# Two-layer block (state-space layer, then FFN): running the FFN of tile t-2 inside the state-space work of tile t

## What is computed

```python
x = x + layernorm(mamba(layernorm(x), W_in, conv_w, conv_b, W_out, A_log, D_param, dt_bias))
x = x + layernorm(ffn(layernorm(x), lut, gate_idx, up_idx, down_idx))

# mamba: proj = u @ W_in.T, split into z, x, B, C, dt
#   xBC = silu(causal_conv(xBC, 4 taps) + conv_b);  dt = softplus(dt + dt_bias);  dA = exp(dt * A)
#   per token: S = S * dA + dt * outer(B, x);  y = S @ C       (8 heads, state 64)
#   y = (y + D_param * x) * silu(z);  return y @ W_out.T
# ffn: w = lut[idx] for three weights (16 levels);  h = silu(x @ gate.T) * (x @ up.T)
#   return h @ down.T                                          (width 512, inner width 1376)
```

## Time and profile before

| | us |
|---|---|
| median of the runs | 1591.49 (1589.11 to 1592.44) |
| span of the profiled execution | 1590.2 |
| TensorE busy | 1431.8 (90%) |
| VectorE busy | 1034.1 (65%) |
| ScalarE busy | 592.3 (37%) |
| GpSimd busy | 541.7 (34%) |

### The profile page before, as it was taken

How to read it: one execution, slowest core, us unless ns; L and a number is a source line. 1 busy time by engine, 2 the same in 40 slices (tenths; PEclk the granted TensorE clock), 3 DMA queues, 4 the chain that set the end, 5 groups by cost and what they waited for, 6 DMA issues and landing times. The chain is left out here.

```text
span 1590.2 us, 23447 instructions
## 1 busy us (share of the span) xinstructions
PE 1431.8 (90%) x7392; PEld 707.9 (45%) x7392; DVE 1034.1 (65%) x2288; ACT 592.3 (37%) x1046; POOL 541.7 (34%) x653
## 2 busy tenths in 40 slices
PE   3798897898979988899886999999999999999998
PEld 1354443443535434445443444444444444444443
DVE  6799797897886978969885535435363545445333
ACT  4365554654645546555453221203020221213020
POOL 1275655556465555665754001010101001010101
PEclk9899998998999999989998999999999999999999
DMA  5011122022121221112201101010100101010000
GB/s 168 1 49 49 49 62 64 15 72 59 38 63 36 62 62 49 59 39 62 62 22 59 53 9 46 1 55 1 54 1 21 34 7 47 1 53 1 27 1 27
DMA packets 37454, 65.22 MB, mean 41 GB/s; under 512 B 5056, under 2 KB 15296, under 8 KB 37312
## 3 DMA queue, kind: packets, MB, share of 16 engines
q1 hardware_dynamic: 35424, 63.47, 12.7%
q10 hardware_dynamic: 1888, 0.03, 0.1%
HBM read 46.71 MB, written 16.78 MB: 40 GB/s over the span
## 5 line engine op out<-in xcount | busy, mean ns | idle before, releaser
L1386 ACT ACTIVATE gtanh<-bank,c_gate_half 128x512 f32<-128x512 f32 (+1 forms) x88 | 60.4, 687 | 537.0 <-PE bank L1421 537.0
L1421 PE MATMUL bank<-xt,ffn_hi 128*128 128x512 f16 (+1 forms) x704 | 213.8, 386 | 13.4 <-DVEq L82 6.7
L991 DVE TENSOR_SCALAR mask<-codes_h 128x416 f16<-128x416 f16 x640 | 215.5, 368 | 1.9
L1421 PE MATMUL bank<-xt_odd,ffn_hi 128*128 128x512 f16 (+1 forms) x704 | 209.4, 379 | 0.0
L1359 POOL TENSOR_TENSOR drstd<-dvar,neg_half 128x1 f32<-128x1 f32 x32 | 17.4, 545 | 481.1 <-DVE dvar L1518 481.1
L828 PE MATMUL bank<-mask,diag 128*128 128x416 f16 x640 | 133.2, 353 | 46.8 <-DVE mask L991 46.6
L1493 DVE SCALAR_TENSOR_TENSOR gsilu<-gtanh,bank 128x512 f32<-128x512 f32 (+1 forms) x88 | 60.5, 687 | 137.6 <-ACT gtanh L1386 137.4
L1421 PE MATMUL bank<-xt,ffn_lo 128*128 128x512 f16 (+1 forms) x352 | 135.7, 385 | 0.0
L1445 PE MATMUL bank<-ffn_hi,h_hi 128*128 128x512 f16 (+1 forms) x352 | 133.5, 379 | 0.0
L1421 PE MATMUL bank<-xt_odd,ffn_lo 128*128 128x512 f16 (+1 forms) x352 | 133.4, 379 | 0.0
L1445 PE MATMUL bank<-ffn_hi,h_lo 128*128 128x512 f16 (+1 forms) x352 | 133.3, 379 | 0.0
(11 more groups left out here) (184 smaller groups left out, 2768.3 us busy)
## 6 DMA issues: line engine op xcount, KB each, us to landing
codes_sb<-codes SPq DMA_DIRECT2D x80, 208.0 KB, 3.5
ut<-u SPq DMA_DIRECT2D x8, 1024.0 KB, 5.7
ures<-u SPq DMA_DIRECT2D x32, 256.0 KB, 2.7
x_scratch<-x SPq DMA_DIRECT2D x32, 256.0 KB, 2.0
xf<-x_scratch SPq DMA_DIRECT2D x8, 1024.0 KB, 5.9
out<-res SPq DMA_DIRECT2D x32, 256.0 KB, 2.0
ffn_hi<-w_in_t SPq DMA_DIRECT2D x4, 580.0 KB, 10.3
ffn_hi<-w_out_t SPq DMA_DIRECT2D x1, 1024.0 KB, 14.5
```

Source lines behind the costliest of these rows:

```text
L991: ins = nc.vector.tensor_scalar(mask[:, n, q, :], codes_h[:, n, :], float(2 * q), None, ALU.is_equal)
L1386: gtanh_ready.inc(nc.scalar.activation(gtanh[0:w, m % 2, :], banks[2 + m % 2][0:w, :], ACT.Tanh, scale=c_gate_half[0:w, :]))
L1421: last = nc.tensor.matmul(bank, wt[:, c0:c0 + w], xts[i][:, half, k, :], start=(k == 0 and n == 0), stop=(k == KC - 1 and n == 2))
```

## The change

The two stages become one. There are ten steps: in step t < 8 the state-space layer of tile t runs, and from t = 2 on the FFN of tile g = t-2 (`LAG = 2`) runs between its parts; steps 8 and 9 (`tail`) are the FFN alone. The 40 units of codes (now 20 in each of steps 0 and 1, each 64 rows of 832 columns) are decoded in the first two steps, with 8 masks of 832 columns a unit. The number of matmuls and of their columns is the same. The order of all queues is written out for each step; no loops are left.

- The conversion of the codes goes from GpSimd to ScalarE (`codes_to_half`, with a bias in place of the lowering on VectorE). The z gate goes from GpSimd and three ScalarE operations to one ScalarE tanh and one VectorE operation (`z_gate`).
- The layer norm of FFN input slices uses the same code as that of `u` (normalise and high part on ScalarE, low part on VectorE); slices are loaded and normalised in pairs.
- Gate, up and down products of the FFN share three banks (3, 6, 7) in strict turns; a turn may start once the turn three before it has been read (`ffn_turn`). The state-space layer keeps banks 0, 1, 2, 4, 5.
- x1 has one buffer; the residual of the FFN is loaded chunk by chunk.
- The end of chunk 3 of a tile (`out_rstd`, `normalise`, `add_residual`) and of the last down product stands in the next step.

In the diff the four `stage` functions are, in this order, those of TensorE, VectorE, GpSimd and ScalarE, each cut to its beginning.

```diff
+LAG = 2
+FFN_BANKS = (3, 6, 7)
+FFN_TURNS = 2 * MB + SUB
...
+                def gate_up(g, m):
...
+                    for side, col0, done in ((0, GATE0, gate_done), (1, UP0, up_done)):
+                        turn = 2 * m + side
+                        if turn < 3:
+                            pe.wait_ge(ffn_turn.sem, ffn_turn.prev(g, (FFN_TURNS - 1, FFN_TURNS, FFN_TURNS)[turn]))
+                        else:
+                            pe.wait_ge(ffn_turn.sem, ffn_turn.now(g, turn - 2))
+                        bank = banks[FFN_BANKS[turn % 3]][0:w, :]
...
+                def stage(t):
+                    scan(t, 0)
+                    if dec:
+                        decode(t, 0)
+                    if ffn:
+                        gate_up(g, 0)
+                        gate_up(g, 1)
+                    if nxt:
+                        slice_transpose(t, "T0")
+                        slice_transpose(t, "T1")
+                    prepare(t, 1)
+                    segment_sums(t, 1)
+                    if dec:
+                        decode(t, 1)
+                    if ffn:
+                        gate_up(g, 2)
+                    transpose_y(t, 0)
...
+                    scan(t, 1)
+                    if dec:
+                        decode(t, 5)
+                    if nxt:
+                        project_dt(t + 1)
+                        project_conv(t + 1, 4)
+                    if ffn:
+                        gate_up(g, 5)
+                    prepare(t, 2)
+                    segment_sums(t, 2)
...
+                    if nxt:
+                        project_z(t + 1, 3)
+                    if dec:
+                        decode(t, 19)
+                    if ffn:
+                        down(g, 3)
...
+                def stage(t):
+                    y_sum(t, 0)
+                    if g >= 1:
+                        down_stats(g - 1, 3)
+                    if t >= 1:
+                        out_stats(t - 1, 3)
+                    if g >= 1:
+                        down_normalise(g - 1, 3)
+                    if ffn:
+                        gate_silu(g, 0)
+                    y_gated(t, 0)
+                    if ffn:
+                        times_up(g, 0)
+                    y_split(t, 0, k + 2 if dec else None)
...
+                def stage(t):
+                    decay_state(t, 0)
+                    if t >= 1:
+                        out_rstd(t - 1, 3)
+                    if g >= 1:
+                        down_rstd(g - 1, 3)
+                    if t >= 1:
+                        add_residual(t - 1, 3)
+                    segments(t, 1)
+                    if g >= 1:
+                        add_output(g - 1, 3)
+                    weights(t, 1)
...
+                def stage(t):
+                    if dec:
+                        codes_to_half(k + 4)
+                    if ffn:
+                        gate_tanh(g, 0)
+                    if nxt:
+                        normalise_slice("u", t + 1, 0, 0)
+                        normalise_slice("u", t + 1, 0, 1)
+                    if ffn:
+                        high(g, 0)
+                        gate_tanh(g, 1)
...
+                    if nxt:
+                        slice_transposed(t, "T0", xt)
+                        slice_transposed(t, "T1", xt)
+                    if t >= 1:
+                        normalise(t - 1, 3)
+                    small(t, 1)
```

More of the change, by code:

```diff
@@ L1 @@
+from collections import namedtuple
 from contextlib import ExitStack
@@ new lines, in sandwich_kernel, with place, pair_buffer, pair_landed @@
+        res_stored = [Signal(sem(f"output_stored{i}"), SUB // 2, step=16, credit=True) for i in range(2)]
+        def place(t, name):
+            b, n = place_of[t, name]
+            return Place(banks[b], shared_filled[b], shared_freed[b], n)
+        def pair_buffer(no):
+            return xs[:, 1, 0:2, :] if no == 1 else ut[:]
+        def pair_landed(no):
+            return u_loaded[1].sem if no == 1 else u_loaded[0].sem, 16 * (no if no > 1 else 1)
+        def conv_sum(i, f):
+            return xs[:, i % HALVES, 0 if f == KC else f, :]
@@ L917, in body @@
                         pe.wait_ge(s_diag, 2 * PAIRS)
                         pe.wait_ge(s_lo, len(PIECES))
-                        decode(t, 0, more)
-                        transpose_y(t, 0)
-                        input_transpose(t, 0, more)
-                        input_transpose(t, 1, more)
-                        scan(t, half, row, 1)
-                        project_out(t, 0)
-                        prepare(t, half, 2)
-                        segment_sums(t, 2)
-                        decode(t, 1, more)
@@ new lines, in decode @@
+                    for j in range(2):
+                        p = take(t, f"D{k}{'ab'[j]}")
+                        for q in range(PAIRS):
+                            if j == 0 and q % GROUP == 0:
+                                pe.wait_ge(s_masks, 2 * count + q // GROUP + 1)
+                            last = nc.tensor.matmul(p.bank[:, 0:COLS], diag[:, q].rearrange("p n m -> p (n m)"),
+                                                    mask[:, n, q, j * COLS:(j + 1) * COLS],
+                                                    start=(q == 0), stop=(q == PAIRS - 1))
+                            if j == 1 and q == GROUP - 1:
+                                last.then_inc(s_masks_used, 1)
+                        last.then_inc(p.filled, 1)
@@ new lines, in segment_sums @@
+                def segment_sums(t, c):
+                    pe.wait_ge(seg_ready.sem, seg_ready.now(t, c + 1))
+                    if t > 0 or c > 0:
+                        pe.wait_ge(y_steps.sem, y_steps.prev(t, YSTEPS * (SUB + c - 1) + 2))
+                    for n in range(2):
+                        last = nc.tensor.matmul(seg_banks[n][:], below[:],
+                                                decay[:, 4 * n:4 * n + 4, :].rearrange("p h t -> p (h t)"),
+                                                start=True, stop=True)
+                    seg_done.inc(last)
@@ new lines, in transpose_y @@
+                def transpose_y(t, c):
+                    p = take(t, f"y{c}")
+                    pe.wait_ge(y_steps.sem, y_steps.now(t, YSTEPS * (c + 1)))
+                    to = p.bank[:].bitcast(F16).rearrange("p (n k t) -> p n k t", n=2, k=KC)
+                    for n in range(2):
+                        for k in range(KC):
+                            last = nc.tensor.transpose(to[:, n, k, :], ysplit[:, n, k * P:(k + 1) * P], ident_h[:])
+                    last.then_inc(p.filled, 1)
@@ new lines, in down @@
+                def down(g, c):
+                    tok = slice(c * P, (c + 1) * P)
+                    turn = 2 * MB + c
+                    pe.wait_ge(ffn_turn.sem, ffn_turn.now(g, turn - 2))
+                    for m in range(MB):
+                        w = MW[m]
+                        if c == 0:
+                            pe.wait_ge(hlo_ready.sem, hlo_ready.now(g, m + 1))
+                        d0 = DOWN0 + m * D
+                        for n, (h, wt) in enumerate(((h_hi, ffn_hi), (h_hi, ffn_lo), (h_lo, ffn_hi))):
+                            last = nc.tensor.matmul(banks[FFN_BANKS[turn % 3]][:], h[0:w, m, tok], wt[0:w, d0:d0 + D],
+                                                    start=(m == 0 and n == 0), stop=(m == MB - 1 and n == 2))
+                    down_done.inc(last)
@@ new lines, in _ @@
+                pe.wait_ge(s_ident, 1)
+                for s in range(SUB):
+                    slice_transpose(-1, f"T{s}")
+                pe.wait_ge(s_lo, 2)
+                project_dt(0)
+                for f in CONV_ORDER:
+                    project_conv(0, f)
+                pe.wait_ge(s_lo, 3)
+                for c in range(SUB):
+                    project_z(0, c)
+                prepare(0, 0)
+                segment_sums(0, 0)
+                for t in range(TILES):
+                    stage(t)
```

2643 lines of the change are left out of this document (1492 added, 1151 removed).

## The result

The changed kernel takes 1673.69 us (1670.83 to 1677.00), the kernel before 1590.3: a ratio of 1.052, 95% interval 1.0506 to 1.0542. Forecast were 1565 us and a gain.

A forecast was written before the change was run, and what follows sets the result against it. TensorE was taken as the bound in stage 2, TensorE and VectorE alternating in stage 1. Head 78, two decoding steps of 153, steps 2 to 9 1173 and end 7.2 gave 1564 of span, forecast 1565 us, range 1522 to 1608.

The forecast's parts named there:

- Steps 0 and 1: The two decoding steps: 129.6 us of TensorE work over an old stage's 85% share, 153 us each, bounds 138 and 178.
- the 166 us: Sign of being wrong: decoding steps passing this length; from there on the slower rival was to decide.
- the same chain of chunks 1 to 3: Output norm, normalise, residual addition, then segments before segment_sums: some 10 us, mostly covered, costing 2 us a step.
- Steps 3 to 6: Steps with state-space and FFN work: 156.5 us of TensorE work plus waits, 171.0 us each.
- The two waits: TensorE idle before a step's first up product, 6.0 us, and before its first segment_sums, about 4 us.
- The first wait: First up product waits for the normalised last down product: 8.6 us chain, 6.0 idle, 7.6 with the lower clock.
- Head and tails: Before the first scan: 78 us, bounds 74 and 84. From step 7 through both tails and the end: 332.9 us.
- Masks of 832 columns: VectorE's decoding masks in steps 0 and 1: 0.30 us each, 48 us a step plus 15 for collisions with GpSimd.
- The faster rival: Decoding steps at 140 us, first wait 4 us, second 3 us; total 1508 to 1535 us; chance 15%.
- The slower rival: Decoding turns on two shared banks run one after another: steps of 177 us, total 1613 us; chance 13%.
- VectorE's order in the FFN steps: VectorE's in-order queue loses 4 to 5 us more in each FFN step, total 1590 us; chance 12%.
- The page on GpSimd's access to SBUF: GpSimd shares SBUF access with some VectorE instructions; FFN beside scan would lengthen chains an estimated 1 us a step.

The follow-up runs named there:

- GpSimd's two reorderings: Changed kernel with GpSimd's segments moved ahead of output norm and residual addition, and its last down power ahead of the output norm's eight steps; 1581.23 us.
- the banks: Decoding turns on the three FFN banks instead of two shared ones: 1655.45 us from the changed kernel, 1555.59 us with GpSimd's two reorderings.
- segments_first: Changed kernel with GpSimd's segments of the next chunk moved ahead of the output norm and residual addition of the chunk before, all four chunks; 1613.68 us.
- weigh_earlier: Kernel with GpSimd's two reorderings, on two shared banks, plus VectorE's weigh of chunk 2 and of the next tile's chunk 0 moved earlier; 1568.18 us.
- all_four_reordered: Changed kernel with GpSimd's segments and down power moved ahead, decoding on the three FFN banks, and VectorE's weigh steps earlier; 1550.66 us.
- fill_first_wait: Changed kernel plus 20 useless matmuls between first gate and first up product, in steps 3 to 6 and 8; 1658.27 us.

## Why the prediction was wrong, point by point

- **Steps 0 and 1: the step that failed.** The old tile's share of 85% was carried over to give 153 us; measured were 184.4 and 191.6, past the 166 us that the prediction had named as a sign of being wrong. It made 70 of the 111 us. The two loads were not the miss: VectorE is busy 118.8 us where 126 were forecast, and TensorE's work was as counted. What failed is the overlap that the share stood for. A share of an old stage says how that stage's order filled; the new one has twenty units of 16 mask matmuls a tile where the old had five. What was left out is what was done for steps 2 to 9: walk TensorE's list and ask at each wait who signals last. The walk was even written down for the FFN steps ("the same chain of chunks 1 to 3"), and the same chain stands in the decoding steps behind less cover: seven waits of `segment_sums`, 27.8 us in all, in steps 0 and 1 of the changed kernel, where the FFN steps had been given 2 us each for it. (They took less: the waits of steps 3 to 6 for segments beyond the first come to 0.4 or 0.5 us a step.) By the runs: 31 and 39 us over the forecast, of which GpSimd's two reorderings give back 3.4 and 10.2, the banks 9.0 and 10.6 on top of them (together 12 and 21); 18 to 19 us a step are left, in which VectorE's and ScalarE's loads count in part. A walk would have found the segments' waits; that it would have found the whole is not shown, since removing these 27.8 us of waits by `segments_first` shortened the two steps by 10.3 only.
- **Steps 3 to 6: mechanism right, a size off.** Forecast 171.0, measured 177.5. The two waits were found with their places and who ends them; their sizes (4.7 and 3.5 for 6.0 and 4.0) were a little too large. All waits together are 14.0 us a step where the sum had 12: the chain of chunks 1 to 3 was oversized too, and some 5 us were not in the sum, 2.6 of them the wait for `weigh`. The larger part of the miss was the lower clock: 1.7 + 0.9 us were given to it, but TensorE's busy time of some 163.5 us is 7 over the 156.5 of full-clock work. In the changed kernel it comes three times a step, once behind that wait for `weigh`. With the waits mended, the busy time is 157.4.
- **The first wait** was sized by 0.75 us for the down power and 3.1 for eight steps; measured 0.54 and 2.4 (812.81 to 815.23, answering to the earlier trace rows). From the end of `scan` to the up product it was 7.5 us in place of 8.6.
- **Head and tails**: 80.7 for 78, 337.6 for 332.9; the first inside its bounds of 74 to 84, the second 1.4% off. The second is nearer than its terms: in step 7 the waits for segments came to 6.2 us where some 9 were given, and the lower clock cost more than given, as in steps 3 to 6.
- **Masks of 832 columns**: forecast 0.30 us from neighbouring rows; eight in a row took 2.37 us (from 109.75), 0.30 each, and one alone 0.37; with collisions the mean in steps 0 and 1 was 0.39, as the 48 + 15 us of the sum. The Trainium skill (VectorE: DVE Perf Modes, the TRN2 errata) gives an estimated 0.28; the trace agrees to within 0.02.
- **The faster rival** (15%) was right on the waits, at 4.7 and 3.5 us where it had 4 and 3, and on GpSimd's first small step, 0.19 us in that wait; it failed with the decoding steps, which it put at 140.
- **The slower rival** (13%) had the right place and sign and asked the right question (over 166 us a step). Its mechanism, turns on two banks, is shown for 10 to 13 us a step. Its price, 24 us a step, was the size that the turns, the GpSimd order and the loop have together, and less than that; its time of 1613 was 61 us too low.
- **VectorE's order in the FFN steps** (12%, 4 to 5 us a step): `weigh` behind the 17 small time steps is such a case, and is shown for 1.0 us a step by `weigh_earlier`. GpSimd's order was worth 13 us a step (177.5 to 164.1); the forecast had 14.5 for its waits over the full-clock work, so it was no rival's matter but the forecast's own.
- **The page on GpSimd's access to SBUF** (the Trainium skill, GPSIMD Engine Reference, Specifications), by which chains would be an estimated 1 us a step longer beside the FFN: in chunk 3 of step 4 the two operations that split y take 1.33 and 2.27 us (948.09 and 949.45) beside GpSimd's addition and `segments` (947.86 to 951.17), and 0.49 and 0.75 in chunk 0, where GpSimd idles. That is 2.4 us in one chunk, so the trace agrees in kind; TensorE had no wait for that split in step 4, so it cost no step length that a row shows.
- **The chances** were too sure: a fifth of the sum (two steps) rested on a share, and the high bound of 178 was itself too low. No case priced the chains of the decoding steps without cover, although those two steps came out 70 us longer together and the forecast gain was 25.

Open: what sets the 171 us of a decoding step after the four edits. Taken out of the changed kernel, TensorE's load counted for 0.1 us a us and VectorE's for 0.4; after the four edits the two together counted for 0.3 and ScalarE's for 0.6. Whether the number of mask buffers or code slots would open the loop was not tried. Nor was it shown how much of the 18 to 19 us left is the lower clock, only that four fillers a unit don't win it back.

## What to carry to other kernels

When work is interleaved, a wait doesn't need to be long in itself: ask of every small engine's queue what stands ahead of the one instruction that the bound engine waits for. Here two moves on GpSimd, which is busy 27% of the time, were worth 92 us, while leaving out three quarters of the decoding's matmuls was worth 6. And size a new phase by walking its queues rather than by the utilisation of an old one: that gave 153 us for steps of 184 and 192. In a dense loop over three engines a load's price showed only when some of it was taken out.

## What the runs showed of the hardware that was not expected

Idle time on TensorE costs more than itself: five waits of 4.2 to 4.9 us filled with useless products gave 15.4 us, although in steps 3 to 6 the product behind them came no earlier. The lower clock was also seen behind an idle time of 2.58 us (882.36, the next 12 matmuls in 4.28 us), a wait that the sum had at nothing, while behind 1.38 us in `all_four_reordered` a product ran at 0.22 us a matmul. Between these the length of the wait alone doesn't tell: the same X product ran at the full clock behind 2.75 us and at the lower one behind 2.58 us in `fill_first_wait`, and at the lower one behind 2.73 us in the changed kernel. What decides is not shown. In the decoding steps the same remedy, in the form tried, did not pay: 14 us of fillers made the steps 7.1 and 5.3 us longer.
